# A four-layer recurrent kernel: the first layer's product and the third layer's low-rank product change places in the loop

## The reference, cut to what matters

```
x = x + (x * ys) @ w0 * d                      # layer 0: no dependence over time
h = tanh(h @ Wh1 + x_t @ Wx1);     x = x + h   # layer 1: a step for each token t
x = x + x @ (base + A_b @ B_b.T)               # layer 2: rank 8, A and B for each sequence b
i, f, o, g = x_t @ Wx3 + h @ Wh3 + b3          # layer 3: LSTM, a step for each token t
c = sigmoid(f) * c + sigmoid(i) * tanh(g);  h = sigmoid(o) * tanh(c);  x = x + h
```

## Time and profile before

| | |
|---|---|
| median of 3 runs | 1129.78 us (1129.75 to 1131.11) |
| profiled execution: time | 1131.51 us |
| profiled execution: span from the first to the last instruction | 1129.7 us |
| mean granted TensorE clock | 0.995 |
| TensorE busy (matmul) | 1092.5 us, 97% |
| VectorE busy | 885.4 us, 78% |
| ScalarE busy | 426.1 us, 38% |
| GpSimd busy | 16.7 us, 1% |

### The profile page before, as it was taken

How to read it: one execution, slowest core, us unless ns; L and a number is a source line. 1 busy time by engine, 2 the same in 40 slices (tenths; PEclk the granted TensorE clock), 3 DMA queues, 4 the chain that set the end, 5 groups by cost and what they waited for, 6 DMA issues and landing times.

```text
span 1129.7 us, 65707 instructions
## 1 busy us (share of the span) xinstructions
PE 1092.5 (97%) x30300; PEld 741.5 (66%) x30300; DVE 885.4 (78%) x2786; ACT 426.1 (38%) x1034; POOL 16.7 (1%) x48
## 2 busy tenths in 40 slices
PE   5779999999999999999999999999999999999997
PEld 3436666676766667676766767666766766676657
DVE  7888878777787877778777777887777778777765
ACT  5884333333333333333333333333333333333322
POOL 1000000000000000000000000000000000000000
PEclk9989999999999999999999999999999999999999
DMA  9991000000000000000000000000000000000000
GB/s 337 404 379 40 23 23 3 22 23 23 22 22 23 6 20 22 23 22 22 23 9 16 23 23 22 23 23 14 12 23 22 23 22 22 13 4 13 13 13 22
DMA packets 24644, 51.96 MB, mean 46 GB/s; under 512 B 4160, under 2 KB 4288, under 8 KB 23344
## 3 DMA queue, kind: packets, MB, share of 16 engines
q1 hardware_dynamic: 23936, 47.49, 11.9%
q10 hardware_dynamic: 432, 0.26, 0.1%
HBM read 39.36 MB, written 8.39 MB: 42 GB/s over the span
## 4 chain that ended last, share of the span: by engine, by line
PE 91%; DMA 4%; DVE 3%; issue 1%; ACT 1%; ACTq 0%; DVEq 0%
PE ps_gates L1563 57%; PE ps_l L1502 8%; PE ps_x L1502 7%; PE ps_l L1615 7%; PE ps_rnn L1615 7%; DMA ring<-in_hw 3%; PE ps_lr L1502 2%; PE ps_z L1532 1%; PE ps_l L1563 1%; DVE big L840 1%; DMA rows<-in_ln_b 1%; PE ps_gates L1471 1%; DVE gates_ring L1126 0%; PE ps_l L1449 0%; DVE b_lo L840 0%
## 5 line engine op out<-in xcount | busy, mean ns | idle before, releaser
L1563 PE MATMUL ps_gates<-big,rows 128*32 128x512 f16 (+1 forms) x6144 | 358.5, 376 | 1.2 <-ACT rows L525 1.2
L1563 PE MATMUL ps_gates<-big,lstm_h 128*32 128x512 f16 (+1 forms) x6144 | 348.9, 376 | 1.0 <-DVE lstm_h L1159 1.0
L1563 PEld LDWEIGHTS ps_gates<-big,lstm_h 128*32 128x32 f16 x6144 | 163.9, 97 | 156.2 <-DVE lstm_h L1159 2.4
L1563 PEld LDWEIGHTS ps_gates<-big,rows 128*32 128x32 f16 x6144 | 161.9, 97 | 141.1 <-issue 1.3
L1126 DVE SCALAR_TENSOR_TENSOR gates_ring<-ps_gates,tile_un,rows 128x256 f32<-128x256 f32 x252 | 110.6, 480 | 94.2 <-PE ps_gates L1563 94.2
L666 ACT ACTIVATE gates_ring<-gates_ring 128x256 f32<-128x256 f32 x128 | 53.4, 417 | 257.6 <-DVE gates_ring L1126 257.6
L1502 PE MATMUL ps_l<-xs,w_hi 128*128 128x128 f16 x1024 | 80.2, 222 | 0.8 <-issue 0.6
L1502 PE MATMUL ps_x<-x,base_hi 128*128 128x128 f16 x1024 | 78.1, 219 | 0.0
L525 ACT ACTIVATE xs<-xsT,tile_s 128x512 f16<-128x512 f32 x32 | 23.1, 721 | 114.6 <-DVE xsT L853 111.1
L1502 PEld LDWEIGHTS ps_l<-xs,w_hi 128*128 128x128 f16 x1024 | 63.1, 100 | 3.1 <-issue 1.6
L1502 PEld LDWEIGHTS ps_x<-x,base_hi 128*128 128x128 f16 x1024 | 62.5, 98 | 1.4 <-issue 1.4
(11 more groups left out here) (221 smaller groups left out, 1710.9 us busy)
## 6 DMA issues: line engine op xcount, KB each, us to landing
ring<-in_hw SPq DMA_DIRECT2D x16, 1024.0 KB, 14.7
xT_sb<-in_xT SPq DMA_DIRECT2D x32, 256.0 KB, 2.8
outT<-late SPq DMA_DIRECT2D x32, 256.0 KB, 2.0
big<-in_wx SPq DMA_DIRECT2D x5, 1024.0 KB, 14.6
big<-in_wh SPq DMA_DIRECT2D x5, 1024.0 KB, 14.3
big<-in_w SPq DMA_DIRECT2D x1, 1024.0 KB, 5.8
big<-in_hw SPq DMA_DIRECT2D x1, 1024.0 KB, 13.4
late<-in_base SPq DMA_DIRECT2D x1, 1024.0 KB, 14.3
```

Source lines behind the costliest of these rows:

```text
L1563: last = nc.tensor.matmul(by_chunk_of_gate(bank[B * j:B * j + B, columns]), of_step, tile_columns(w, j)[:, gates], start=start, stop=stop, ...
```

## The change

Three streams are reordered inside the main loop; no instruction is added or removed there.

TensorE: `l0(c)` moves out of the first gap and behind `l1(r + 2)` in the second; `gates_x(t + 2)`, the input part of LSTM step t+2, which was there, moves to the first gap, in front of `x3_low_rank(a1)`, and `l1(r + 1)` stands in front of both.

VectorE: `x1(c)` and `x1_low(c)` move from the first gap to the second, behind `x3_low(a1)`. `tile_scales`, `tile_undo` and `xs` move from the second gap to the third, behind `gate_scales(i)`. `xs_low` and `x_magnitude`, which were there, move to the fourth, in front of `x2(i)` and `x2_low(i)`.

ScalarE: `x3_high(a1)` and `x1_high(c)` stand behind `rnn(r + 1)`, and `xs_high(c + 1)` behind `rnn(r + 2)`, in front of the activations of step t+3.

```diff
 # ScalarE
                 zm_high(a1)
-                x1_high(c)
                 low_rank_share(a1)
-                x3_high(a1)
                 lstm(t + 1)
                 rnn(r + 1)
+                x3_high(a1)
+                x1_high(c)
+                lstm(t + 2)
+                rnn(r + 2)
                 if in_l0(i + 1):
                     xs_high(c + 1)
-                lstm(t + 2)
-                rnn(r + 2)
                 lstm(t + 3)
                 rnn(r + 3)
                 x2_high(i)
 # VectorE
                 lstm_out(t)
-                x1(c)
                 if i == LAG:
                     x_magnitude(LAG + 2, 0)
                 x3_first(a1)
-                x1_low(c)
                 lstm_sums(t + 1)
...
                 x3_low(a1)
-                if in_l0(i + 1):
-                    tile_scales(i + 2, 1, 0)
-                    tile_undo(i + 2, 1, 0)
-                    xs(i + 2)
+                x1(c)
+                x1_low(c)
                 lstm_sums(t + 2)
...
                 gate_scales(i)
                 if in_l0(i + 1):
-                    xs_low(i + 2)
-                if i + 3 < TILES:
-                    dve.wait_ge(m_spread, i + 3)
-                    x_magnitude(i + 3, 0)
+                    tile_scales(i + 2, 1, 0)
+                    tile_undo(i + 2, 1, 0)
+                    xs(i + 2)
                 lstm_sums(t + 3)
...
                 lstm_out(t + 3)
+                if in_l0(i + 1):
+                    xs_low(i + 2)
+                if i + 3 < TILES:
+                    dve.wait_ge(m_spread, i + 3)
+                    x_magnitude(i + 3, 0)
                 x2(i)
                 x2_low(i)
 # TensorE
                 z(a1)
-                l0(c)
                 x3_base(a1, range(KC))
+                l1(r + 1)
+                gates_x(t + 2)
                 x3_low_rank(a1)
-                l1(r + 1)
                 lstm(t + 1)
                 rnn(r + 1)
                 l1(r + 2)
-                gates_x(t + 2)
+                l0(c)
                 gates_x(t + 3, (0,))
                 lstm(t + 2)
```

## The result

The changed kernel takes 1151.35 us (median of 4 runs, 1150.75 to 1151.46), the kernel before in the same session 1129.8: a ratio of 1.0187, with an interval from 1.0174 to 1.0199. It is 21.5 us slower. Forecast was slower, 1147 with a range of 1137 to 1154.

What follows compares the result with a forecast made beforehand. TensorE's matmuls were taken to bound the kernel, so a reorder could only make a wait: 27 x 0.64 = 17.3 us at `z`, added to the median of 1129.8, gave 1147.1 us, range 1137 to 1154.

Steps and rivals of the forecast that it cites:

- What bounds the kernel: Main loop: TensorE never waits, its matmuls leave 0.76 us open in 300; reordering frees nothing but can make a wait.
- The sum of a pass does not change: TensorE in the loop: the swap takes 0.10 us from the first gap and gives it to the second.
- Second gap: VectorE: `x1` and `x1_low` make `lstm_sums(t+2)` 0.59 us late; cover of 0.55 leaves 0.04.
- Third gap: `xs_high` on ScalarE stands before step t+3's sigmoid, making everything up to `lstm_out(t+3)` 0.50 us late.
- Fourth gap: VectorE: `xs_low` and `x_magnitude` add 1.26 us before `x2`; `x2_low` ends 1.76 later, `z` waits 0.64.
- The start of `z`: TensorE: after `x2_low` ends, 0.06 us to the weight load and 0.12 to the first matmul, at 661.43 instead of 660.79.
- 27 passes: Of the loop's 29 passes, 27 hold both moved instructions, so `z` waits 27 x 0.64 = 17.3 us.
- half the wait: At `z`: `xs_high` finds room before the sigmoid, only VectorE's 0.18 counts, wait 0.32, 1138.4 us; 12 in 100.
- The rival of the full lengths on VectorE: Fourth gap: the two moved instructions count 1.42 us, `z` waits 0.80, kernel 1151.4 us; 3 in 100.
- The clock: TensorE: the wait lets its clock fall in places from its level of 1.00; 2 in 100.
- The longer chain: Second gap: `x1` takes over 0.3 us more than worked out, using up its cover; 1155 us; 11 in 100.
- a pass 0.6 longer: Main loop, sign in the profile after: each pass lasts 0.6 us longer than before.

Runs made afterwards that it cites:

- e1: The changed kernel with `xs_low` and `x_magnitude` moved behind `x2_low` on VectorE: 1141.7 us, ratio 1.0106.
- e7: The changed kernel with TensorE's order as in the kernel before and `xs_low` and `x_magnitude` behind `x2_low` on VectorE: 1129.4 us, ratio 0.9995.
- e3: The kernel before with `l1(r + 1)` between `l0(c)` and `x3_base` on TensorE: 1135.95 us, ratio 1.0053.
- e5: The kernel before with `l0` halved and the three parts of `l1(r + 1)` set between its halves and around `x3_base`: 1148.8 us, ratio 1.0168.
- e2: The changed kernel with only TensorE's order put back as in the kernel before: 1143.1 us, ratio 1.0119.
- e4: The changed kernel with `xs_high` behind the activations of LSTM step t+3 on ScalarE: 1146.8 us, ratio 1.0151.
- e6: The changed kernel with TensorE's first gap regrouped as `z`, `l1`, `gates_x(t + 2)`, `x3_base`, `x3_low_rank`: 1153.2 us, ratio 1.0206.
- e8: The changed kernel with `l1` directly behind `z` on TensorE, and `xs_low` and `x_magnitude` behind `x2_low` on VectorE: 1150.4 us, ratio 1.0183.
- e9: The kernel before with `l1(r + 1)` directly behind `z` on TensorE: 1139.5 us, ratio 1.0084.

## Why the prediction was right, and where it was not

The direction, the place and the mechanism of the first loss were right; that the sum, 17.3 us against 21.5 measured, came near was luck, because two errors went against each other: the forecast term was worth 9.7 us (e1), and one of 12.3 us was missing.

- **What bounds the kernel** (TensorE, a pass as long as its matmuls; nothing to free, a wait to be made): right, but for the next point. e7 shows that VectorE's and ScalarE's new order costs nothing once `z` doesn't wait.
- **"The sum of a pass does not change"**: wrong. This is the step that failed. It holds for the matmuls but not for their order: two more changes of array shape and back a pass cost 0.45 us, 12 to 13 us in all (e1 against e7, which differ in TensorE's order alone: 1141.7 - 1129.4 = 12.3). Rows that could have warned were in the trace of before. In its last stretch the low-rank product stands behind an LSTM step, the step takes 2.69 us from start to start and not 2.59 (1093.06 to 1095.75), and the weight load idles:

```profile
1095.75 0.12 PEld L1502 LDWEIGHTS ps_lr<-zm,b_hi 128*128 128x128 f16 x2 [0.42 <-issue]
```

The one pair in each pass of the loop shows it too:

```profile
628.27 0.34 PE L1532 MATMUL ps_z<-a_hi,x 128*32 128x64 f16 x16
...
634.58 0.19 PE L1502 MATMUL ps_lr<-zm,b_lo 128*128 128x64 f16 x1
634.70 0.41 PE L1615 MATMUL ps_l<-wx_hi,x 128*32 128x128 f16 x16
```

The last third of `z` takes 0.27 until `l0` starts (at 628.54), where the third in front of it takes 0.14, and the last matmul of the low-rank product takes 0.12, where others take 0.03: 0.13 and 0.09, together the 0.22 of e3 and e5.
- **Second gap**: the chain through `x1` came as worked out (`lstm_sums(t+2)` 0.66 behind `x1_low`, 656.60 to 657.27), and its cover held. The prediction had 0.04 us of delay that the cover would not take up; but the gap had become 5.10 and not 4.89, by the shape changes, and no delay was left over: `rnn_turned` starts 0.37 behind the cell's last instruction (658.84 to 659.21), 0.16 later than where it needn't wait for `rnn(r + 2)` (0.21). With TensorE's old order the cover is too short (e2).
- **Third gap**: the order of events was right, ScalarE's `xs_high` in front of the sigmoid. The size, 0.50, was too large: measured from TensorE's `rnn(r + 2)`, the sigmoid came 6.88 behind it (658.32 to 665.20) against 6.47 in the kernel before (647.08 to 653.55), 0.41 later; what followed was only 0.31 later, because ScalarE's next activation, with its input there, followed after 0.31 (665.20 to 665.51) and not after 0.39 as before. So `x2` came 11.75 behind `rnn(r + 2)` (658.32 to 670.07), where it came 10.18 behind it in the earlier trace rows: 1.57 later, 1.26 of it the two moved instructions. e4 puts ScalarE's own part at 0.17 at `z`.
- **Fourth gap**: the two moved instructions cost 1.26 us as forecast (668.81 to 670.07), with the overlap of 0.08 seen before. Their full lengths, 1.42, which the prediction took from the Trainium skill, VectorE: DVE Perf Modes, section "The DRAIN you can't avoid", didn't come; the section itself says that an operation that is not held starts earlier.
- **The start of `z`**: I added 0.06 and 0.12 from the write to the first matmul. The matmul started 0.06 behind the write. The 0.12, taken from another kind of matmul, was too much; why these follow closer is open. Together with the third gap, 0.64 became 0.32, and this term 17.3 became about 9 (e1: 9.7).
- **27 passes**: right; the waits count 27, and none in the pass after.
- **Rivals**: half the wait was in fact the size of this term (0.32), by parts of two causes and not by the one named. The rival of the full lengths on VectorE gave 1151.4, the measured time almost to the tenth; that is chance, since the two instructions took 1.26 and not 1.42. The clock did not move (1.00 in the stretch). The longer chain didn't come in the changed kernel; in e2 the cover of the second gap did run out, by 0.16.
- **What would be seen**: "a pass 0.6 longer" is 0.77; "no wait at line 1563" is right. That there would be a wait at line 1502 was not foreseen.

## What to carry to other kernels

Where TensorE is full, an order costs something by itself: put products that use the array in the same way next to one another, and count the changes of shape of a new order (0.22 us there and back here, 29 times a pair). That has a limit: three products of short matmuls in a row (e6, e8, e9) ran through their instructions faster than new ones came, and this cost 8 to 14 us, more than the 6.4 us that a pair of changes costs. Work moved on another engine is free only up to the first result behind it that the full engine wants: take the time by which that result is early (1.30 us here) as the budget of everything put in front. And read a full engine's loss from the distances between starts, not from its busy share, which fell by one point while 21 us were lost.

## What the runs showed of the hardware

- A change from products on 32-column tiles to products over the full array and back costs 0.218 to 0.220 us (e3, e5), about 0.1 each way, with no semaphore involved. Behind matmuls with 512 columns (`gates_x` in front of the low-rank product) the one way took the same 0.10.
- TensorE can stand still with all operands there, because the next block of its own instructions is late. In this kernel the blocks hold 256 instructions, and all 70 such stops in eight runs lie at one place of a block, 1.2 to 1.7 us behind the landing of the last packet. A run of 144 short matmuls with their loads in about 1.9 us goes with stops of up to 1.1 us in e9 and 1.6 us in e8, in more than half of the passes. With 96 in the run, seven of the 29 passes of the kernel before are 0.1 to 0.6 longer than the rest. The stop can fall within a group of equal matmuls.
- At a change of shape the first weight load starts together with its matmul and not ahead of it. Behind matmuls with 512 columns a full-array load idles 0.42 us (11.9 us over 28 passes).
